# Moving two products of the joining layer into the gap ahead of the fourth layer, and reordering the first chunk of a graph attention chain

## The reference, cut to what matters

```python
def _gat_layer(h, adj_mask, W_l, lw, lb, a):
    Wh = h @ W_l
    u, v, c = Wh @ lw[:C] @ a, Wh @ lw[C:] @ a, lb @ a
    e = jax.nn.leaky_relu(u + v.T + c, negative_slope=0.2)
    att = jax.nn.softmax(jnp.where(adj_mask, e, NEG_INF), axis=1)
    return jax.nn.elu(att @ Wh)

h, outs = x, [x]                       # block 2
for i in range(2):
    h = 0.2 * x + 0.8 * _gat_layer(h, mask, W[i], lin_w[i], lin_b[i], attn[i])
    outs.append(h)
joined = jnp.concatenate(outs, axis=-1) @ mlp_w + mlp_b
```

## Time and profile before

| what | us |
|---|---|
| median of three timed executions | 585.03 |
| the three | 585.03, 584.64, 595.99 |
| the profiled execution, its own time | 580.28 |
| its span, first to last instruction | 578.4 |
| mean granted clock of TensorE over the span | 0.988 of full speed |

### The profile page before, as it was taken

The page is one execution under the profiler, slowest core; times in us unless marked ns, Lnnn a source line. Parts: engine busy times, 40 slices in busy tenths (PEclk is TensorE's granted clock), DMA queues, the critical chain, the costliest instruction groups (busy, mean ns, idle before and its releaser), DMA issues.

```text
span 578.4 us, 7918 instructions
## 1 busy us (share of the span) xinstructions
PE 529.5 (92%) x3300; PEld 202.4 (35%) x3300; DVE 380.3 (66%) x551; ACT 263.3 (46%) x297; POOL 30.2 (5%) x32
## 2 busy tenths in 40 slices
PE   6888987998998998998888999999889999999997
PEld 5422222343223343323233223245334344333332
DVE  4888689548979637989765989637977983100000
ACT  3479964534665543665543755444234772000000
POOL 3300000211000100000100000021100000000000
PEclk9879999999999999999999999999999999999999
DMA  8977000000000000000000000000000000000000
GB/s 309 409 280 275 4 1 1 0 2 1 1 0 1 2 0 2 1 1 0 1 1 2 0 2 1 0 1 1 1 1 1 0 1 2 0 1 1 0 19 18
DMA packets 5635, 19.43 MB, mean 34 GB/s; under 512 B 608, under 2 KB 608, under 8 KB 5600
## 3 DMA queue, kind: packets, MB, share of 16 engines
q1 hardware_dynamic: 5600, 18.93, 8.9%
HBM read 18.40 MB, written 0.52 MB: 33 GB/s over the span
## 4 chain that ended last, share of the span: by engine, by line
PE 63%; DVE 23%; ACT 6%; issue 4%; DMA 3%; POOL 1%; SPq 0%; DVEq 0%; ACTq 0%
PE PROD L793 11%; DVE X L1361 10%; PE X L1062 10%; PE PROD L1062 9%; PE X L785 7%; PE S L813 6%; ACT big L471 4%; DMA big<-in_adjT 3%; PE X L1053 2%; DVE tops L1625 2%; DVE big L1373 2%; PE M L648 1%; DVE nadj L1475 1%; PE M L747 1%; DVE big L1370 1%
## 5 line engine op out<-in xcount | busy, mean ns | idle before, releaser
L471 ACT ACTIVATE big<-X,v 128x1024 f32<-128x1024 f32 x128 | 141.6, 1114 | 100.5 <-PE X L785 100.1
L1361 DVE SCALAR_TENSOR_TENSOR X<-wB,v,aB 128x1024 f32<-128x1024 f32 x128 | 163.4, 1293 | 27.6 <-ACT big L471 26.3
L793 PE MATMUL PROD<-big,Wh 128*64 128x512 f32 x512 | 134.3, 605 | 1.9 <-ACT big L471 1.7
L785 PE MATMUL X<-nadj,bigI 128*64 128x512 bf16 x512 | 77.9, 383 | 19.6 <-DVE X L1361 19.3
L785 PEld LDWEIGHTS X<-nadj,bigI 128*64 128x64 bf16 x512 | 25.3, 109 | 102.3 <-DVE X L1361 73.2
L813 PE MATMUL S<-big,onesf 128*32 128x512 f32 x400 | 53.3, 604 | 2.4 <-DVE big L1373 2.4
L793 PEld LDWEIGHTS PROD<-big,Wh 128*64 128x64 f32 x512 | 31.1, 136 | 52.2 <-issue 30.3
L1062 PE MATMUL PROD<-big,Wh 128*64 128x512 f32 x128 | 30.6, 594 | 0.0
L528 ACT ACTIVATE big<-nadj 128x1024 fp8e4<-128x1024 bf16 x26 | 26.3, 1053 | 9.0 <-DVE nadj L1475 9.0
L398 POOL TENSOR_TENSOR rr<-var,mhalf 128x8 f32<-128x8 f32 x8 | 14.5, 1818 | 298.7 <-DVE var L1222 298.7
L1062 PE MATMUL X<-big,Wh 128*64 128x512 f32 x128 | 28.6, 595 | 0.0
(11 more groups left out here) (307 smaller groups left out, 597.2 us busy)
## 6 DMA issues: line engine op xcount, KB each, us to landing
big<-in_adjT SPq DMA_DIRECT2D x28, 512.0 KB, 7.5
aB<-in_adjT SPq DMA_DIRECT2D x4, 512.0 KB, 7.5
cst<-in_cst SPq DMA_DIRECT2D x1, 537.0 KB, 7.5
x<-in_xT SPq DMA_DIRECT2D x1, 512.0 KB, 3.7
out<-x SPq DMA_DIRECT2D x2, 256.0 KB, 2.0
late<-in_late SPq DMA_DIRECT2D x1, 272.5 KB, 5.8
cst<-in_cst SPq DMA_DIRECT2D x1, 263.0 KB, 2.8
```

Of the source, the lines that this page charges most:

```text
L471: act.activation(prob[:, t % U, :], X[t % 2][:], ACT.Exp, bias=v2[l % 2][:, k:k + 1]).then_inc(p_ready, 1)
L785: last = pe.matmul(X[t % 2][feat(side), hh * BANK:(hh + 1) * BANK], bigI[:, feat(side)], nadj[:, k, half_cols(c, hh)], start=False, stop=T ...
L793: last = pe.matmul(PROD[c][feat(hh), :], Wh[l % 2][:, k, :], prob[:, t % U, hh * BANK:(hh + 1) * BANK], start=k == 0, stop=k == NB - 1)
L1361: dve.scalar_tensor_tensor(X[t % 2][:], wB[:, cols(c)], v8[l % 2][:, k:k + 1], aB[:, cols(c)], ALU.max, ALU.add).then_inc(x_written, 1)
```

## The change

It does three things.

1. The products of h0 and h1 leave `mlp(c)` and become `skip_terms(c)`. That of c = 0 goes into the gap ahead of the fourth layer, that of c = 1 behind `w_rows` of the fourth layer, in banks of their own. VectorE adds them with the bias to x by a new `skip_rows(c)`: for c = 0 behind the third layer's end, for c = 1 behind the second exponents of the fourth layer. `mlp_rows` is left with a plain addition. In the gap `features` moves ahead of the last five early levels; filler goes from 4 to 3 there, and from 17 to 8 behind `w_rows` (in another bank).
2. The adjacency's transfers 18 to 21 go to slots 0 to 3, and the later ones are dealt anew.
3. In the first layer two fillers are put behind each of the levels 9, 10, 12 and 13, and the filler behind `w_broadcast(1)` goes from 4 to 6. In the loop over the first chunk the last two level blocks (14, 15 of chunk 1) go ahead of the sums of pair p = 5, `shift_products` goes from p = 6 (behind the products) to the end of p = 5, and in the last pair the two masks of the next chunk go ahead of the sums.

```diff
--- before.py
+++ after.py
@@ -234,6 +234,7 @@
         rp_ready = sem("rp_ready")
         e_ready = sem("e_ready")
         mlp_psum = sem("mlp_psum")
+        skip_psum = sem("skip_psum")
         c2_psum = sem("c2_psum")
         cg_ready = sem("cg_ready")
         sq2_ready = sem("sq2_ready")
@@ -284,7 +285,7 @@
 
         ADD_BEHIND = ({3: (1,), 6: (4,), 8: (5,), 12: (10,)}, {3: (1,), 5: (2, 3), 7: (4,)})
         ADDS = 4
-        SLOT_OF = [n % SLOTS for n in range(NB)] + [(7, 8, 4, 5, 6)[j % 5] for j in range(NB)]
+        SLOT_OF = [n % SLOTS for n in range(NB)] + [(7, 8, 0, 1, 2, 3, 4, 5, 6, 7, 8, 4, 5, 6, 7, 8)[j] for j in range(NB)]
 
         block = ctx.enter_context(nc.Block())
         N_C = 6
@@ -332,7 +333,7 @@
             return sum(1 for m in range(n + 1) if SLOT_OF[m] == SLOT_OF[n])
 
         def by_dve(n):
-            return n < NB and n % 3 == 0
+            return n % 3 == 0 if n < NB else False
 
         def copies_by_dve(n):
             return sum(1 for m in range(n + 1) if by_dve(m))
@@ -345,6 +346,9 @@
 
         def again(c):
             return (M, PROD[0])[c]
+
+        def skip_bank(c):
+            return (X[1][:, BANK:CH], M[:])[c]
 
         def sums_of(n):
             return EB[n % 2] if n >= 6 else EA[n % 2]
@@ -551,8 +555,9 @@
                 for k in range(NB):
                     exponential(l, 0, k)
                     if l == 0 and k % 2 and k < 12:
-                        adjacency8(NB + 3 + k)
-                        adjacency8(NB + 4 + k)
+                        for n in (NB + 3 + k, NB + 4 + k):
+                            if not by_dve(n):
+                                adjacency8(n)
                     if l == 0 and k == 13:
                         shift_rows(0, 2, 4)
                     if k == 3 and l:
@@ -742,6 +747,8 @@
                 for jb in range(CB if l else 0, NB):
                     if l == 0:
                         chunk_levels(0, jb)
+                        if jb in (9, 10, 12, 13):
+                            repeat(X[1][:, BANK:CH], 2)
                         continue
                     for q in range(4):
                         last = pe.matmul(M[WIN * q:WIN * (q + 1), :], level[:, jb, :],
@@ -833,14 +840,19 @@
 
             def mlp(c):
                 n = NCH * 3 + c
-                pe.wait_ge(ld_late, 16)
                 pe.wait_ge(p_copied, n + 1)
-                for k, src in enumerate((h0, h1)):
-                    pe.matmul(EB[c][:], mw[:, k, :], src[:, c, :], start=k == 0, stop=False)
                 pe.wait_ge(t_ready, n + 1)
-                pe.matmul(EB[c][:], mw[:, 2, :], tb, start=False, stop=False)
+                pe.matmul(EB[c][:], mw[:, 2, :], tb, start=True, stop=False)
                 pe.wait_ge(e_ready, n + 1)
                 pe.matmul(EB[c][:], mw[:, 2, :], eo, start=False, stop=True).then_inc(mlp_psum, 1)
+
+            def skip_terms(c):
+
+                pe.wait_ge(ld_late, 16)
+                pe.wait_ge(h0_ready, c + 1)
+                pe.wait_ge(h_ready, c + 1)
+                pe.matmul(skip_bank(c), mw[:, 0, :], h0[:, c, :], start=True, stop=False)
+                pe.matmul(skip_bank(c), mw[:, 1, :], h1[:, c, :], start=False, stop=True).then_inc(skip_psum, 1)
 
             def centre_mlp(c):
                 pe.wait_ge(x_new, 2 * 2 + c + 1)
@@ -900,12 +912,16 @@
             for l in range(GAT):
                 top_levels(l)
                 w_rows(2 * l + 1)
-                repeat(M, 17 if l else 8)
+                if l == 3:
+                    skip_terms(1)
+                    repeat(PROD[0], 8)
+                else:
+                    repeat(M, 17 if l else 8)
                 if l == 0:
                     chunk_levels(1, 0)
                     chunk_levels(1, 1)
                     w_broadcast(1)
-                    repeat(PROD[0], 4)
+                    repeat(PROD[0], 6)
                 pe.wait_ge(nv_ready, 4 * (l + 1) if l else 2)
                 mask(l, 0, 0)
                 mask(l, 0, 1)
@@ -924,17 +940,19 @@
                         if l == 0 and c == 0:
                             products(0, 0, k)
                             products(0, 0, k + 1)
-                            if p == 6:
+                            for i in range(2):
+                                if p < NB // 2 - 1:
+                                    mask(0, 0, k + 2 + i)
+                                else:
+                                    mask(0, 1, i)
+                            if p == 5:
+                                chunk_levels(1, NB - 2)
+                                chunk_levels(1, NB - 1)
+                            sums(0, 0, k + 1)
+                            for jb in range(4 + k if p else 2, 6 + k if p < 5 else 0):
+                                chunk_levels(1, jb)
+                            if p == 5:
                                 shift_products(0, 2, 4)
-                            if p < NB // 2 - 1:
-                                mask(0, 0, k + 2)
-                                mask(0, 0, k + 3)
-                            sums(0, 0, k + 1)
-                            for jb in range(4 + k if p else 2, 6 + k if p < 6 else 0):
-                                chunk_levels(1, jb)
-                            if p == NB // 2 - 1:
-                                mask(0, 1, 0)
-                                mask(0, 1, 1)
                             continue
                         for i in range(2):
                             products(l, c, k + i)
@@ -994,10 +1012,11 @@
                     repeat(X[0], 2)
                 if l == 2:
                     early_levels(l + 1, 0, 3)
+                    skip_terms(0)
                     w_broadcast(2 * l + 2)
+                    features(2 * l + 3)
                     early_levels(l + 1, 3, CB)
-                    features(2 * l + 3)
-                    repeat(X[0], 4)
+                    repeat(X[0], 3)
             def key_block(c, t, b, side=slice(0, P)):
                 return slice(0, KPAD), c, t, slice(b * P + side.start, b * P + side.stop)
 
@@ -1414,10 +1433,14 @@
                 signal(dve.tensor_tensor(h0[:, c, :], g[:, c, :], EB[c][:], ALU.mult), h0_ready, c + 1)
 
             def mlp_rows(c):
+                dve.wait_ge(mlp_psum, c + 1)
+                ins = dve.tensor_tensor(x[:, c, :], x[:, c, :], EB[c][:], ALU.add)
+                signal(ins, x_new, 2 * 2 + c + 1)
+
+            def skip_rows(c):
                 dve.wait_ge(ld_late, 16)
-                dve.wait_ge(mlp_psum, c + 1)
-                ins = dve.scalar_tensor_tensor(x[:, c, :], EB[c][:], mb, x[:, c, :], ALU.add, ALU.add)
-                signal(ins, x_new, 2 * 2 + c + 1)
+                dve.wait_ge(skip_psum, c + 1)
+                link(dve.scalar_tensor_tensor(x[:, c, :], skip_bank(c), mb, x[:, c, :], ALU.add, ALU.add))
 
             def norms(c):
 
@@ -1476,7 +1499,7 @@
 
             def convert(n):
                 dve.wait_ge(ld_adj[SLOT_OF[n]], 16 * uses(n))
-                if n < NB - 1:
+                if n != NB - 1:
                     mask_words(n)
                 if by_dve(n):
                     dve.tensor_scalar(adj[:, n % NB, cols(n // NB)], slot(n), 0, None, ALU.is_gt,
@@ -1543,7 +1566,7 @@
                     if l == 0:
                         if k <= 10:
                             for n in range(NB + (5 if k > 1 else 4) + k, NB + 6 + (k if k else -1)):
-                                mask_words(n)
+                                convert(n)
                         if k == 13:
                             top_codes(2, slice(P // 2, P))
                         if k == NB - 1:
@@ -1557,6 +1580,8 @@
                         (target_second if k in (9, 13) else target_first)(l, 1, k // 10)
                     if k == 1 and l == 2:
                         activated(1, 1)
+                    if k == 1 and l == 3:
+                        skip_rows(1)
                     if k == 11 and l == 2:
                         input_rows(1)
                 for k in range(NB):
@@ -1613,6 +1638,7 @@
                     shifted(l, 1)
                 if l == 2:
                     activated(l, 1)
+                    skip_rows(0)
                 if l < 2:
                     clip(2 * l + 3)
                     variance(2 * l + 3)
```

## The result

The changed kernel takes 574.84 us (median of four, 574.34 to 577.41), the kernel before beside it 584.84. The ratio of the means is 0.9839, 95% interval 0.9803 to 0.9876: 9.4 us less, 1.6%. That is clear of the interval, but short of the 2% that the forecast took as its bound. One execution of the kernel before (595.99) and one of e2 (1333.51) were disturbed; the ratios leave them out, the medians count them.

The account below looks back on a forecast made before the run. TensorE, busy for 92% of the span, was taken to bound the kernel where it is the late engine. Terms -1.1 - 1.1 - 0.7 + 0.1 - 1.7 - 0.6 = -5.1 us, applied to the median 585.03, gave 579.9 us, range 575 to 584.5.

Parts of the forecast that it names:

- Start of the first layer, -1.1: First layer's levels and spreading: added filler holds TensorE's full clock, spreading takes 1.1 instead of 2.06; -1.1 us together.
- End of the first chunk, -1.1: First chunk's last pairs: levels ahead of sums, spreading ahead of products; only TensorE's waits of 0.61 and 0.46 credited, -1.1 us.
- Slots, nothing alone and 0.3 in company: First layer's adjacency transfers: earlier slots worth nothing alone, about 0.3 us with the other edits, inside the start's 1.1.
- Gap, -0.7: Ahead of the fourth layer: `skip_terms(0)` just fits 1.99 us of idle TensorE and features come earlier; -0.7 us.
- `skip_rows(1)`, +0.1: Fourth layer: takes 0.76 in VectorE's wait of 0.76, with a step of semaphore behind it; +0.1 us.
- Rival 3: Gap ahead of the fourth layer: `skip_terms(0)` starts late and pushes the row's spreading, nothing gained there; 580.6 us, chance 0.09.
- Joining layer, -1.7, -0.5 and -0.1: `mlp(0)` loses four instructions, -1.7 us; `mlp(1)` then waits for `tb`, -0.5; `mlp_rows` as plain addition, -0.1.
- I apply the sum to the median: Whole kernel: -5.1 us taken from the median 585.03, though the profiled execution took 580.28, 4.75 less for an unshown reason.
- Rival 1: First layer's start: the clock falls all the same, +0.4 instead of -1.1, giving 581.4 us; chance 0.20.
- Rival 2: First layer: gains are absorbed later in that layer, only the fourth layer's -2.9 is left, 582.1 us; chance 0.13.
- the rule of the Trainium skill: First layer's clock fall: the rule ties falls to long idle gaps, so filler between the levels would not cure it.

Follow-up runs that it names:

- e2: The kernel before with only the first-layer filler added (eight matmuls between the levels, two behind the row's spreading): 582.2 us, ratio 0.9990.
- e8: The changed kernel again, unedited, beside the kernel before on the chip of the later runs: 575.87 us, ratio 0.9890.
- e3: The changed kernel without the added first-layer filler (0 instead of 8 between the levels, 4 instead of 6 behind the spreading): 576.36 us, ratio 0.9890 to the kernel before.
- e10: The kernel before with only the first-layer filler added, run once more for its trace: 581.54 us, ratio 0.9974.
- e5: The kernel before with only the new order in the first chunk: 580.96 us, ratio 0.9972.
- e12: The kernel before with the h0 and h1 products left out of the joining layer and eight fillers in the gap ahead of the fourth layer: 578.84 us, ratio 0.9942.
- e7: The changed kernel with the old transfer slots: 575.93 us, ratio 0.9897 to the kernel before.
- e13: The changed kernel with 13 instead of 8 fillers ahead of the fourth layer's first mask: 574.74 us, ratio 0.9871 to the kernel before.
- e4: The kernel before with only the products of h0 and h1 moved, first layer's filler, slots and order as before: 577.83 us, ratio 0.9922.
- e1: The kernel before, run again with no edit: 581.78 us, ratio 0.9995.
- e11: The kernel before with the h0 and h1 products left out of the joining layer, the wait of 2 us in the gap left open: 579.83 us, ratio 0.9949.
- e9: The kernel before with eight fillers in the wait of 1.99 us ahead of the fourth layer: 581.28 us, ratio 0.9982.

## Why the prediction was right, and where its size was off

1. *Start of the first layer, -1.1.* In the profiled pair -1.25 from the first level to aB, on the path foreseen: 0.95 in the spreading (1.13 for 2.08; 1.0 was forecast) and 0.30 ahead of it (0.1 was forecast). The pair is of kind A in both members, and that was luck: in kind B there is no fall at 33.5 to prevent, and the filler costs 0.7 where the fall comes at 28 (e8 against e3). Not foreseen either: 0.4 to 0.5 of an early aB is lost in the chunk behind, with filler as without. Over all executions the term is small, 0 to -1.5 (e2, e10).
2. *End of the first chunk, -1.1.* This term was mis-sized: -1.9 (e5 against e12, e7 against e10). I credited TensorE's two waits only, because it is nearly full. Its visible waits shrink by no more than 0.5 (0.62 and 0.46 gone, 0.57 new). But the way over ScalarE and VectorE, by which the next chunk's start hangs, is shorter by 2.0: the second chunk's aB comes 38.74 behind the first in e12 and 36.70 in e5. Which of TensorE's smaller steps carry the rest is not assigned. In the pair the chunk shows -1.78: about -1.9 for the order, -0.35 for the slots (e7 against after) and +0.4 to 0.5 lost behind the early aB.
3. *Slots, nothing alone and 0.3 in company.* 0.36 in e7 against e13; alone they were not tried.
4. *Gap, -0.7, and `skip_rows(1)`, +0.1.* -0.70 and +0.08 (e4). The moved products and the earlier `features` were not tried apart. Rival 3, an overflow, did not come: 299.14 to 301.12 for the products, and L712 at 301.19.
5. *Joining layer, -1.7, -0.5 and -0.1.* -1.72 in chunk 1, -0.4 (the pair) to -0.5 (e4) in the rest, for -0.6. For the second part the wait for `tb` took over as said: ahead of L845 the chain goes over VectorE's L1418 up to 390.19.
6. *"I apply the sum to the median."* This step failed. I left the 4.75 us between the profiled execution and the median as a constant of the kernel. It is none: before it was 4.75 and later 2.2 (582.47 against 580.28), after it was 0.3 and later 1.3 (574.84 and 575.87 against 574.57). So the median gained 4.5 more than the trace at first, and 0.9 more later. The sum of the trace, -5.1 forecast and -5.7 measured, is right for two executions with the same kind of start and falls alike elsewhere. The profiled execution of the kernel before was among its quickest: only 5 of 73 took less than 581. One cause is shown with price and cure: the fall behind the wait of 2 us in the gap, 1.1 to 1.5 us when it happens (e1, e11), 1.0 by the ratio when the wait is filled (e9). Part 1 fills that wait with its own products. Executions with much of the lower level are also gone: a mean clock of 0.982 or less stands at 20 of 73, against none of the ten timed ones of the changed kernel (0.990 to 1.0), though this comparison mixes the two kinds. I had also read the mean clock of 0.988 as a low level "for a short time only"; the stretch ahead of the first recorded change isn't counted in it.

Of the 4.5 of part 1, 2.9 are its trace and 1.0 is e9's; 0.6 is left, within the intervals. What stays open is the 9.4 of the first measurement against 6.4 later. The changed kernel took about the same time in both (574.84, 575.87); the kernel before took 584.6 to 585.0 at first, which is what its executions with the most falls took later. The clock of those first executions isn't recorded, so this is argued and not shown.

Rival 1 (the clock falls all the same) was refuted for the fall it named (none of three traces of kind A), and came true in the form that it had allowed for: the fall can lie elsewhere. Rival 2 was refuted by e5: 213.12 to 213.29 us between the first chunk and the end of layer 3 in every trace, whatever came ahead. As for the rule of the Trainium skill ("TensorE: Matmul & The Clock Gate", "Why this matters for your kernels"), that falls come behind long idle gaps: the traces here don't agree with it as a full account. The fall at 33.5 us came behind pauses of at most 0.86 (the last longer one, 2.27, had ended 6.4 us earlier), e1's fall came behind one wait of 2 us among matmuls, and the same wait of 2.5 us ahead of the levels was followed by a fall in e8 and by none in e10. The length of the gap alone did not decide.

## What to carry to other kernels

Work of a later stage whose inputs are ready early belongs in a wait of TensorE: here it was paid twice, once by what left the full stage, and once because the clock no longer fell behind the filled wait. A profiled execution prices the moves to a tenth of a us, but not how often the clock falls. Ask where the profiled execution stands among the timed ones, and read more than one trace, before carrying its gain over to the median. The mean clock is no substitute: 0.988 stood at 580.3 and at 583.3 us. And compare traces of the same kind of start, or the difference of the starts is taken for the work of the edit, as with e10. Filler in front of work that itself waits is a bet on where the fall lies: it gained 1.25 in one place and lost 0.7 in the other.

## What the runs showed of the hardware that I had not expected

- The same program has its falls of the clock in different places from one execution to the next (all up to 570 us). Kind A: at 13 and 33.5 us (before, e4), the same and 306 (e1), 12 and 35.5 (e9), 12 to 13 only (after, e13), 12.5 and 316 (e7). Kind B: at 28 only (e3, e8), 28 and 305 (e11), 28 and 45 (e12), 28, 45 and 403 (e5), none (e10).
- A recorded clock of 1.00 ahead of the first recorded change doesn't mean full speed: the matmuls of L692 took 427 ns there in e10 and 276 ns later.
- A fall is not always costly: the one at 13 to 20 us is in the two fastest traces (after, e13), and with it the levels begin 0.4 to 1.1 us earlier than in the traces without it.
- In all thirteen traces of the table the 213 us from the first chunk to the end of layer 3 agree within 0.17 us, and no fall was seen there: the differences come from the few places where TensorE waits.
